# SyncE reads the experts' numbers and issues the second weight transfer of every tile; ScalarE keeps the first

## What is computed

```python
x = x + ss2d(group_norm(x))          # depthwise conv, then a scan over 2304 pixels, 256 x 16 states
t = tokens(x)
t = t + linear_attention(layer_norm(t))
# mixture of experts: 8 experts, the best 2 of each token
logits = x @ Wg;  top_w, top_idx = softmax(top_k(logits, 2))
h = x @ W1[e];  g = x @ W3[e] + b3[e]
out = sum_e C[e] * ((silu(h) * g) @ W2[e])
```

## Time and profile before

| what | value |
|---|---|
| median of 3 runs | 3860.7 us (3859.01 to 3863.91) |
| the profiled execution, its own time | 3844.76 us |
| its span, first to last instruction | 3842.9 us |
| granted TensorE clock, mean of the span | 0.916 |
| busy: PE, DVE, POOL, ACT | 3126.6, 3057.3, 2822.3, 2347.0 us |
| stretch of the six images' experts with ACT's weights | 945 to 3430 us |

### The profile page before, as it was taken

The page is one execution under the profiler, slowest core; times in us unless marked ns, Lnnn a source line. Parts: engine busy times, 40 slices in busy tenths (PEclk is TensorE's granted clock), DMA queues, the critical chain, the costliest instruction groups (busy, mean ns, idle before and its releaser), DMA issues.

```text
span 3842.9 us, 68512 instructions
## 1 busy us (share of the span) xinstructions
PE 3126.6 (81%) x17390; PEld 1997.4 (52%) x17390; DVE 3057.3 (80%) x5492; ACT 2347.0 (61%) x5132; POOL 2822.3 (73%) x2969
## 2 busy tenths in 40 slices
PE   5687888778889888898889888898889888777772
PEld 3233344335556555664556555564556555557772
DVE  2698989998898798888898788888898788944541
ACT  3354576456857766666856767576766767566331
POOL 1465667696758887788968888688968889786534
PEclk9788899789989998999989999999999999888996
DMA  3965656465769678786868768785878867875883
GB/s 85 222 148 132 150 130 171 109 164 136 217 175 258 178 189 213 214 226 155 233 181 240 190 180 223 197 247 142 234 187 237 209 169 211 222 205 186 256 261 117
DMA packets 420320, 730.00 MB, mean 190 GB/s; under 512 B 56203, under 2 KB 313814, under 8 KB 417750
## 3 DMA queue, kind: packets, MB, share of 16 engines
q1 hardware_dynamic: 327190, 534.99, 54.7%
q10 hardware_dynamic: 74304, 152.60, 12.9%
q0 software_dynamic: 18432, 37.93, 3.6%
HBM read 596.93 MB, written 100.07 MB: 181 GB/s over the span
## 4 chain that ended last, share of the span: by engine, by line
POOL 25%; issue 24%; PE 21%; DVE 16%; ACT 7%; DMA 3%; SPq 1%; ACTq 1%; POOLq 1%; DVEq 0%; PEldq 0%
POOL prod L731 12%; DVE state L1652 6%; PE ps_conv L934 5%; PE ps_main L1000 4%; DVE ps_x L1639 3%; POOL got L854 3%; POOL rows_in L831 2%; POOL hidden L843 2%; PE ps_y L1014 2%; PE ps_h L1106 2%; PE ps_x L948 1%; DMA dt_rep<-dt_dram 1%; POOL big_k L808 1%; DMA w_up<-in_w_exp 1%; PE ps_g L1149 1%
## 5 line engine op out<-in xcount | busy, mean ns | idle before, releaser
L731 POOL TENSOR_TENSOR prod<-state,c_rep 128x384 f32<-128x384 f32 x1536 | 1532.7, 1007 | 588.8 <-DVE state L1652 570.6
L1652 DVE TENSOR_TENSOR_SCAN state<-dt_rep,carry,ps_x 128x384 f32<-128x384 f32 x1280 | 1285.6, 1004 | 0.0
L1639 DVE TENSOR_TENSOR ps_x<-ps_x,db_rep 128x384 f32<-128x384 f32 x1536 | 853.1, 555 | 243.4 <-PE ps_x L948 227.9
L1265 ACT ACTIVATE dt_rep<-dt_rep,vecs 128x768 f32<-128x768 f32 x768 | 717.6, 935 | 141.2 <-DMA dt_rep<-dt_dram 101.0
L948 PE MATMUL ps_x<-x_stack,copy 96*128 96x384 bf16 x1536 | 533.8, 350 | 314.7 <-DVE state L1652 309.5
L934 PE MATMUL ps_conv<-gx,w_conv 128*128 128x384 f32 x1728 | 688.0, 505 | 7.8 <-DVE parts L1669 4.6
L948 PEld LDWEIGHTS ps_x<-x_stack,copy 96*128 96x128 bf16 x1536 | 153.8, 100 | 687.1 <-DVE state L1652 495.1
L934 PEld LDWEIGHTS ps_conv<-gx,w_conv 128*128 128x128 f32 x1728 | 300.0, 194 | 216.7 <-issue 128.7
L854 POOL DMA_INDIRECT got<-rows_out,row_of x288 | 279.8, 972 | 132.9 <-DMA rows_out<-u_out 73.0
L1014 PE MATMUL ps_y<-prod,fold 128*32 128x384 f32 x3072 | 359.6, 543 | 19.7 <-POOL prod L731 14.0
L831 POOL DMA_INDIRECT rows_in<-big_u,row_of x288 | 289.4, 1005 | 101.8 <-issue 96.2
(11 more groups left out here) (272 smaller groups left out, 5416.7 us busy)
## 6 DMA issues: line engine op xcount, KB each, us to landing
dt_rep<-dt_dram SPq DMA_DIRECT2D x384, 768.0 KB
w_up<-in_w_exp ACTq DMA_DIRECT2D x258, 384.0 KB
w_down<-in_w_exp ACTq DMA_DIRECT2D x258, 193.5 KB
w_up<-in_w_exp SPq DMA_DIRECT2D x86, 384.0 KB
x_stack<-parts SPq DMA_DIRECT2D x576, 48.0 KB
u_in<-rows_in SPq DMA_DIRECT2D x344, 64.5 KB
rows_out<-u_out SPq DMA_DIRECT2D x344, 64.0 KB
dt_dram<-dt SPq DMA_DIRECT2D x192, 96.0 KB
```

The costliest lines, as they stand in the source:

```text
L731: pool.tensor_tensor(prod[:, k % HS, :], state[:, k % HS, :], c_rep[:, c % 2, :], ALU.mult).then_inc(s_prod.sem, 1)
L1265: act.activation(dt_rep[:, g % XS, q:q + 2, :], dt_rep[:, g % XS, q:q + 2, :], ACT.Exp, scale=decay_rate).then_inc(s_decay.sem, 2)
L1639: dve.tensor_tensor(x_n, x_n, db_rep[:, c % 2, :], ALU.mult).then_inc(s_inflow.sem, 1)
L1652: dve.tensor_tensor_scan(state[:, k % HS, :], dt_rep[:, g % XS, q, :], ps_x[k % XB][:, 0:T], init, ALU.mult, ALU.add).then_inc(s_state.sem, 1)
```

## The change

SP gets the reading of the expert's number and the issue of `w_down` for all images; ACT still reads the number and issues `w_up`. Tiles 0 to 2 keep their steps. For tile u + 3 SP's step is the fifth after PE's start of tile u (`T_SPW`), with a wait for `read(m, f"g{u}")`; ACT did it at the second, after its own work on `g{u}`. For the last two images the transfers stay as they are, and `apart` adds a semaphore instruction between the wait and the reading.

```diff
+T_SPW = 5
             def weights(m, u):                       # SP
                 e = sp.value_load(expert_of[0:1, parity(m), u:u + 1], min_val=0, max_val=NE - 1)
                 tall = a["w_exp"][bass.ds(e, 1)].rearrange("o p f -> p (o f)")
-                sp.dma_start(w_up[:, u % WA, :], tall[:, 0:2 * F]).then_inc(s_up[u % WA].sem, 16)
-                if u >= WB:
+                if late(m):
+                    sp.dma_start(w_up[:, u % WA, :], tall[:, 0:2 * F]).then_inc(s_up[u % WA].sem, 16)
+                if late(m) and u >= WB:
                     due(sp, s_low, m - (B - 2), u - WB + 1)
                 sp.dma_start(w_down[:, u % WB, :], tall[:, 2 * F:3 * F + MF]).then_inc(s_down[u % WB].sem, 16)
...
                 for u in range(WA):
-                    if late(m) and t == T_W + 2 * u:
+                    if t == T_W + 2 * u:
...
-                u = tile_of.get(t - 2)
-                if late(m) and u is not None and u + WA < NU:
-                    sp.wait_ge(*full(m, f"g{u}"))
+                u = tile_of.get(t - (2 if late(m) else T_SPW))
+                if u is not None and u + WA < NU:
+                    sp.wait_ge(*(full if late(m) else read)(m, f"g{u}"))
+                    apart()
                     weights(m, u + WA)
...
             def weights(m, u):                       # ACT
                 act.dma_start(w_up[:, u % WA, :], tall[:, 0:2 * F]).then_inc(s_up[u % WA].sem, 16)
-                act.dma_start(w_down[:, u % WB, :], tall[:, 2 * F:3 * F + MF]).then_inc(s_down[u % WB].sem, 16)
```

## The result

| | before | changed |
|---|---|---|
| median of 9 runs | 3860.7 us | 3875.61 us |
| lowest to highest | 3853.99 to 3864.35 | 3873.5 to 3888.41 |
| profiled execution, its own time | 3844.76 us | 3873.5 us |

The ratio is 1.0043 with a 95% interval of 1.0032 to 1.0054: 12 to 21 us slower, 16.6 us in the middle. Forecast was 3857 us with a range that ended at 3873. One of the twelve executions of e15 took 8970 us for a reason that isn't known, and its ratio leaves it out.

What follows compares the result with a forecast made beforehand. PE, DVE and POOL taking turns were held to bound the kernel, ACT seldom late. The terms -7 + 2.4 + 0 + 0.6 = -4 us, set against the 3860.7 us median, gave 3857 us, range 3844 to 3873.

Steps and rivals of the forecast that it cites:

- What bounds the kernel: From 945 to 3430 us PE, DVE and POOL take turns; ACT is seldom late, its gains mostly becoming longer waits.
- Part 1: ACT loses 258 issues of 0.51 us: 7 us gained, half of the upper bound of 14.8 us.
- The sign given for this part: ACT's waits for `ps_g` and `ps_h` grow by most of 132 us; if much less, ACT counted for more.
- Part 2, the costs of SP: SP's reading and issue take about 1.17 us per tile, 302 us in 258 tiles, mostly in SP's idle time.
- The cover elsewhere: At 188 `dt_rep` issues SP waited for the scan, 676.4 us in all, so added work there costs nothing.
- Where SP has no cover: Steps 69 to 72: `dt_rep` issued 2.34 us later, mostly hidden by full DMA engines; 0.4 us per image, 2.4 us lost.
- The rival of the queue: `w_down` moves ahead of `dt_rep` in SP's queue: 17 us at six places, 3871 us in all; chance 0.08.
- The rival of SP's lateness: Later `dt_rep` issues at steps 69 to 72 delay ACT: 14.0 us lost there, 3870 us in all; chance 0.15.
- the second rival: SP becomes late for `dt_rep` at steps 69 to 72, which ACT hands on: 3870 us; chance 0.15.
- Part 3: `w_down` issued three steps later on SP's queue still arrives in time, hidden: 0 us.
- the 7.3 us of room: Tightest place, at the 38th tile: time from SP's issue of the 41st tile's `w_down` to ACT's need of it.
- Part 4: Last two images: the added semaphore instruction, 0.06 us, counts about ten times on the chain, 0.6 us lost.

Runs made afterwards that it cites:

- e15: e11 run again, on the chip of e13 and e14: ratio to the kernel before 0.9973.
- e6: The kernel before, with a second reading of the expert's number on ACT at each of the 258 tiles: ratio 1.0025, 9.6 us slower.
- e14: e11 with a second reading of the expert's number on ACT at each of the 258 tiles: ratio to the kernel before 0.9985.
- e4: The changed kernel, with SP's reading and `w_down` of tiles 0 to 2 at steps 61, 62, 65 and no added semaphore instruction: ratio 0.9995.
- e11: The kernel before, only ACT's loading of tiles 0 to 2 moved to steps 61, 62, 65 from 67, 69, 71: ratio 0.9965, run again 0.9973.
- e9: e4 with ACT's reading and `w_up` of tiles 0 to 2 at the earlier steps too: ratio to the kernel before 0.9978, run again 0.9976.
- e13: e9, with SP's reading and `w_down` of the other 40 tiles only in steps that begin with a `dt_rep`, behind it: ratio 0.9966.
- e5: The kernel before, with SP reading the number twice at steps 67, 69, 71 and issuing nothing; ACT keeps both transfers: ratio 1.0016.
- e7: The kernel before, with only tiles 0 to 2 of images 0 to 5 having their reading and `w_down` on SP: ratio 1.0035.
- e10: e7, with SP's reading doubled and the `w_down` transfers behind the `dt_rep` of steps 68 and 72: ratio to the kernel before 0.9997.
- e1: The changed kernel without the added semaphore instruction of the last two images: ratio to the kernel before 1.0035.

## Why the prediction was wrong, step by step

**What bounds the kernel** held: PE, DVE and POOL take turns, ACT is seldom late, and it mattered where the chain runs through something of ACT's.

**Part 1**, 7 us of gain: not contradicted, and not measured by itself. An added slot costs 5 to 10 us (e6, e14), and if a removed one is worth as much, half of the bound was a fair size. But in the changed kernel it doesn't come out: with the loss of the first three tiles and of the late loop taken away, 2 us were left (e4), and e11, without the move, is not behind e9 or e13. If 7 us is right, something at the other 40 tiles takes about 5 us back. e13 gives 4 us for their place against `dt_rep`, without the waits to go with it; this stays open. The sign given for this part failed too: ACT's waits for `ps_g` and `ps_h` grew by 16.8 us together, not by most of 132. That need not mean that ACT counted for more, as the sign had it. An issue that ACT makes while it would be waiting for PE anyway lies inside that wait; what shrank is the idle time before `dt_rep` that is put down to ACT's own issuing, from 40.2 to 3.9 us.

**Part 2, the costs of SP**: 1.17 us per tile was right (1.16 us measured), and so were the place and the delay of 2.3 us there. The cover elsewhere held as well, since SP found itself waiting for the scan 186 times at `dt_rep`, as against 188 in the earlier trace rows, and 561.3 us instead of 676.4:

```profile
SPq L578 <- DVE state L1654: 561.3, 186, 9.9
```

**Where SP has no cover** is the step that failed. I took 0.4 us of the 2.34 for each image because the DMA engines were full until `dt_rep` landed, reasoning that the same bytes have to be moved in either kernel. For the later issue alone that was nearly right: in e5 `dt_rep` went out 2.1 us later and landed 2.0 us sooner after its issue. But the sum had nothing for the transfers themselves. The bytes are the same, but the engines were full of bytes from several queues, and those in `dt_rep`'s own queue are moved ahead of it. The change put three transfers of 0.96 us into just that queue, one ahead of the `dt_rep` of step 68 and two ahead of that of step 72. Measured: 1.0035 for e7, some 13.5 us, where the sum had 2.4 us, and 0.9997 for e10 with the same transfers behind. The rival of the queue, 17 us at the six places and 3871 us in all, had the right mechanism and nearly the right size, and I gave it 0.08. The rival of SP's lateness, 14 us, is the smaller part, 6 us by e5's time with 2 to 10 in its interval, and in e5's trace the waits for these `dt_rep` grew by only 1 us; how the 6 us arise is open. I kept the two apart as alternatives, though nothing excluded both at once; the upper end of the range was made from one alone, and the time lay 2.6 us beyond it. Against the second rival I had also misread the chain of before: `dt_rep` was not the one transfer in it, since `u_in` is there too, with 10.80 us at 3331.58.

**Part 3** held: `g_sb` waited for `w_down` twice in the stretch, 1.0 us in all. That was still closer than I took it to be: one `w_down` of 9.28 us is in the chain at 3353.04, and such a one would not fit into the 7.3 us of room.

**Part 4**, 0.6 us: e1 makes it 3 us, within its interval also 0. The upper end, the 80 tiles that got the instruction times 0.06 us, would be 5 us. I had counted the times that the chain reached `w_up` itself, but when SP runs through several tiles in a row every tile's instruction can count. In the chain of the changed kernel near the end, one tile's `weights` follows another on SP before the transfer that is waited for:

```profile
3785.80 0.27 SPq L633
...
3786.50 0.35 SPq L636
...
3787.03 0.34 SPq L639
...
3788.44 0.27 SPq L633
...
3789.14 4.39 DMA w_up<-in_w_exp
```

## What to carry to other kernels

When a transfer changes its queue, look for what is issued right behind it in the new one, and whether somebody already waits for that. Here full DMA engines hid an issue that came 2.1 us later, but not the transfers put ahead in the same queue, about 1.1 us of later landing each (e7 against e10). Before easing an engine, look at the place where it waits for a transfer and move the crowd in front of that away; here three steps in a table did more than 258 issues taken off ACT. And two rivals that can be true together belong in one upper bound.

## What was not expected of the hardware

With the issue equally late, three transfers of 193.5 KB per image cost 0.38% of the time between standing ahead of a 768 KB transfer in its queue and standing behind it, and about half of that between ahead and another queue. With the engines full, a 768 KB transfer issued 2.1 us later landed at the same time, 17.3 us after the issue of step 68 both before and in e5. A reading of a register on ACT, at 258 tiles, costs 9.6 us (e6), though ACT is idle for 783 of 2485 us.
